# One attention and feed-forward layer on one core: the query products of a half together in slot 5, the key products in slot 6

## What is computed

```python
x1 = x + attention(layernorm(x), ctx)        # q = xn @ w_q, k = ctx @ w_k, v = ctx @ w_v
                                             # softmax(q k^T / 8) v, heads joined, @ w_o + b_o
y  = layernorm(x1)
g  = top2(softmax(y @ gate)), normalised
out = x1 + sum_e g_e * (relu(y @ W1_e + b1_e) @ W2_e + b2_e)
```

## Time and profile before

| | |
|---|---|
| median of 3 runs | 1590.04 us (1586.91 to 1590.92) |
| profiled execution | 1587.79 us, span 1586.0 us |
| busy in the span | PE 1547.8 us, PEld 1444.4, DVE 1265.9, ACT 1102.6, POOL 883.1 |
| granted clock of TensorE, mean | 0.995 of 2.4 GHz |
| DMA | 161.65 MB, mean 102 GB/s |

### The profile page before, as it was taken

One profiled execution on the slowest core, in us unless ns is written; L12 is line 12 of the kernel. 1 busy time (PEld: TensorE's weight loads), 2 busy tenths in 40 slices (PEclk: granted clock), 3 DMA queues, 4 the chain that ended last, 5 costly groups with the idle time before them and its releaser, 6 DMA issues.

```text
span 1586.0 us, 45542 instructions
## 1 busy us (share of the span) xinstructions
PE 1547.8 (98%) x14030; PEld 1444.4 (91%) x14031; DVE 1265.9 (80%) x3796; ACT 1102.6 (70%) x3357; POOL 883.1 (56%) x946
## 2 busy tenths in 40 slices
PE   8999999999999999999999999999899999999997
PEld 7888899989899988889998989989799999999997
DVE  4788888888888888888888888877788777777775
ACT  5777676677776767767767777667667677777774
POOL 2455655655555665565565555555456555555556
PEclk9999999999999999999999999999999999999999
DMA  6533222232222232322223222221799755555554
GB/s 213 156 93 93 73 73 80 80 113 86 80 73 76 84 93 93 93 73 73 80 83 110 88 78 73 77 74 57 250 238 256 144 88 87 88 85 91 84 84 60
DMA packets 123276, 161.65 MB, mean 102 GB/s; under 512 B 18208, under 2 KB 101280, under 8 KB 122976
## 3 DMA queue, kind: packets, MB, share of 16 engines
q1 hardware_dynamic: 77776, 105.59, 22.1%
q0 software_dynamic: 26816, 37.32, 13.4%
q10 hardware_dynamic: 18640, 18.19, 4.4%
HBM read 93.61 MB, written 67.44 MB: 102 GB/s over the span
## 4 chain that ended last, share of the span: by engine, by line
issue 41%; POOL 24%; DVE 9%; DMA 9%; PE 9%; DVEq 3%; ACT 2%; POOLq 1%; ACTq 1%
DMA out<-stage_room,number 9%; POOL lists L680 7%; POOL prob L687 6%; PE bank_a L1453 4%; DVE hid L1381 3%; DVE stage_room L1398 3%; POOL stage_room L729 2%; POOL stage_room L725 2%; POOL shifted L663 2%; POOL mean_var L666 1%; DVEq L1393 1%; POOL rstd L666 1%; DVEq L1372 1%; PE bank_s L1471 1%; PE bank_v L1486 1%
## 5 line engine op out<-in xcount | busy, mean ns | idle before, releaser
L687 POOL TENSOR_TENSOR prob<-prob,inv 128x512 f32<-128x512 f32 x256 | 298.3, 1165 | 462.0 <-DVE inv L978 460.7
L795 ACT ACTIVATE prob<-bank_s,low 128x128 f32<-128x128 f32 x1024 | 363.2, 377 | 58.4 <-DVE low L973 58.4
L973 DVE TENSOR_REDUCE low<-bank_s 128x4 f32<-128x512 f32 x256 | 175.4, 685 | 120.9 <-PE bank_s L1471 120.8
L753 POOL DMA_INDIRECT out<-stage_room,number x142 | 230.6, 1624 | 53.6 <-issue 53.1
L788 ACT ACTIVATE probt<-bank_t 128x512 f32<-128x512 f32 x256 | 153.6, 600 | 116.2 <-PE bank_t L1460 116.1
L795 ACT ACTIVATION_READ_ACCUMULATOR prob<-bank_s,low 128x1 f32 x1024 | 221.5, 216 | 0.0
L1089 DVE SCALAR_TENSOR_TENSOR stage_room<-xin,wo_t 128x256 f32<-128x256 f32 x480 | 201.2, 476 | 0.0
L823 ACT ACTIVATE ot_h<-bank_v 128x512 fp32r<-128x512 f32 x128 | 77.3, 604 | 147.6 <-PE bank_v L1486 147.6
L907 ACT ACTIVATE hidt_h<-hid 128x512 fp32r<-128x512 f32 x142 | 89.7, 632 | 114.4 <-DVE hid L1381 112.1
L680 POOL DMA_INDIRECT lists<-rows,slot x128 | 149.3, 1166 | 34.1 <-issue 34.1
L1460 PE MATMUL bank_t<-ident,prob 128*128 128x128 f32 x1024 | 161.8, 281 | 5.5 <-POOL prob L687 4.7
(11 more groups left out here) (235 smaller groups left out, 4795.5 us busy)
## 6 DMA issues: line engine op xcount, KB each, us to landing
stage_room<-lists ACTq DMA_DIRECT2D x67, 265.0 KB, 2.9
halves<-stage_room SPq DMA_DIRECT2D x32, 512.0 KB, 4.4
homes<-halves SPq DMA_DIRECT2D x16, 1024.0 KB, 6.8
xin<-in_x SPq DMA_DIRECT2D x32, 256.0 KB, 2.8
xraw<-in_x_t SPq DMA_DIRECT2D x32, 256.0 KB, 3.0
stage_room<-in_x SPq DMA_DIRECT2D x32, 256.0 KB, 3.4
stage_room<-in_w SPq DMA_DIRECT2D x32, 256.0 KB, 4.4
out<-stage_room SPq DMA_DIRECT2D x32, 256.0 KB, 2.9
```

The lines of the kernel that those rows point to most:

```text
L687: pool.tensor_tensor(prob[:, n % 4, :, :], prob[:, n % 4, :, :], wide(inv[:, n % 4, :], P), ALU.mult).then_inc(s_norm.sem, 1)
L753: pool.indirect_dma_start(out, bass.IndirectOffsetOnAxis(ap=number[:, u, b:b + 1], axis=0), ysum[:, u, b, :], None, compute_op=ALU.add).th ...
L795: e = act.activation(prob[:, n % 4, h, :], bank_s[n % 2][:, h * P:(h + 1) * P], ACT.Exp, bias=low[:, n % 4, h:h + 1], scale=-1.0, accum_ou ...
L973: dve.tensor_reduce(low[:, n % 4, :], bank_s[n % 2][:, :].rearrange("p (h k) -> p h k", h=4), AX.X, ALU.min).then_inc(s_low.sem, 1)
```

## The change

The slots of the next pair's products are written in another order. Slot 5 had one query and one key product, and so had slot 6; now slot 5 has both query products and slot 6 both key products. The banks follow the position in the slots: the second product of slot 5 has bank 1 and the first of slot 6 bank 2, as before. No operation is added, left out or changed in size.

```diff
@@ -117,8 +117,8 @@
         [("k11", CUR), ("q11", CUR)],
         [("o1", FROM0)],
         [("v10", CUR), ("v11", CUR)],
-        [("q00", NEXT), ("k00", NEXT)],
-        [("q01", NEXT), ("k01", NEXT)],
+        [("q00", NEXT), ("q01", NEXT)],
+        [("k00", NEXT), ("k01", NEXT)],
         [("v00", NEXT), ("f0", BOTH), ("v01", NEXT)],
     ]
 
@@ -140,7 +140,7 @@
     A_BANKS = 4
 
     BANK_OF = {"q10": 0, "k10": 1, "o0": 2, "k11": 3, "q11": 0, "o1": 1, "v10": 2, "v11": 3,
-               "q00": 0, "k00": 1, "q01": 2, "k01": 3, "v00": 1, "f0": 0, "v01": 2}
+               "q00": 0, "q01": 1, "k00": 2, "k01": 3, "v00": 1, "f0": 0, "v01": 2}
```

## The result

The changed kernel takes **1571.76 us** (median of 5 runs, 1570.14 to 1572.39) against 1589.75 (5 runs, 1585.59 to 1590.92): the ratio is 0.9892, with a 95% interval of 0.9877 to 0.9908, or 18.0 us less. The forecast was 1574, range 1569 to 1583. The profiled execution took 1570.14 us, 17.65 less than that of before; its span is 1568.4 us, 17.7 less (1586.04 to 1568.38).

What follows compares the result with a forecast made beforehand. TensorE, busy 98% of the span, was taken to bound the kernel. 30 stalls x 0.47 (0.23 + 0.24) = 14.1, plus 1.4 in iteration -1, made 15.5 us: median 1574, range 1569 to 1583.

Steps and rivals of the forecast that it cites:

- The stall: Slot 5: TensorE at k00's first matmul (L1514) waits for VectorE's low part of the context (L1203), 0.52 us, 30 times.
- What is late next: Scores of slot 6 wait for unit 5's exponentials, plus 0.15 us; start no earlier than 633.30, so slot 5 gives 0.23.
- the new wait: Ahead of slot 6's scores, TensorE waits for the exponentials of unit 5: 0.05 us in place of the old wait.
- The sign that the prediction set: TensorE's waits after: small ones of L1471 for ScalarE's L795, under 0.1 us each and below 4 us in all.
- the twin case: Exponentials don't hold slot 6's scores: 0.52 us per iteration, 17.0 in all, 1573; chance 0.80 together with the forecast.
- Slot 6: k00 has ten matmuls where q01 had twelve: 0.24 us less per iteration.
- Room behind it: Between unit 7's last exponential and the next slot 0 scores 0.7 us is left, so the gain survives.
- Iteration -1: Once: q01 covers all of k00's 1.40 us stall for the k weights, gaining 1.4 us.
- Iteration 29: No stall at k00; TensorE waits 2.98 us for unit 3's normalisation, GpSimd being late; left as it is.
- The pace of ScalarE: Rival: ScalarE's row of work sets the pace; 0.23 us per iteration, 8.3 in all, 1581.7; chance 0.08.
- the moved wait: Rival: the new wait at slot 6's scores takes all; time as before, 1589 to 1590; chance 0.07.
- The rival in which VectorE's low part falls under a GpSimd instruction: L1203 under GpSimd in every iteration costs 1.53 us each through the shared port lock; 32 slower, 1620; chance 0.05.

Runs made afterwards that it cites:

- e1: Kernel before, with VectorE's low part of the context moved ahead of the second copy of v products in slot 4; 1581.61 us, ratio to before 0.9960.
- e4: Changed kernel with q01 moved from slot 5 to the head of slot 6; 1615.87 us, ratio to before 1.0181.
- e2: Changed kernel with VectorE's low part of the context behind slot 5's minimum and reciprocal, except in iteration -1; 1568.85 us, ratio to before 0.9886.
- e10: Changed kernel in which q01 of iteration -1 also waits for the k weights; 1572.54 us, ratio to before 0.9907.
- e9: Kernel before, with VectorE's low part of the context behind slot 5's minimum and reciprocal; 1607.04 us, ratio to before 1.0123.
- e3: Mirror of the change, both key products in slot 5 and both query products in slot 6; 1634.22 us, ratio to before 1.0296.

## Why the prediction was right

*The stall.* 0.52 from start to start, met at 30 places, and all of it gone: shown by the waits after, in which L1514 is no longer named. That it would not be worth 0.52 was the point of the working, and e1 shows it apart: 0.24 measured, 0.23 worked out.

*What is late next.* The exponentials of unit 5, with 0.15 from ScalarE to TensorE, taken from a single case in iteration 0. After the change the distance is 0.14 to 0.15 all along; e4 and e1 show the same limit under other loads, e2 lifts it. The size of the new wait was off: 0.05 was forecast, and e2 gives 0.14. The sign that the prediction set, waits under 0.1 in TensorE's list, did not come either: the list has none. Most of the miss is q01's 1.60 from its first matmul to the values: it took 622.97 - 621.44 = 1.53. I had scaled it from k00's 1.36, and k00 came out of a stop, where the first matmul is followed by the next only 0.20 later (631.15 and 631.35 in the trace before), not 0.12. These 0.08 belong to the stop too, 0.52 + 0.08 = 0.60, and e1 splits the 0.60 into a new wait of 0.36 and a gain of 0.24. The miss cost the sum nothing, because the exponentials decide, but it made the twin case, scores not held, too small: 0.52 per iteration, where e2 gains 0.61 over the kernel before.

*Slot 6.* 0.24 for two matmuls fewer. 0.47 in all were forecast per iteration; 13.08 / 28 = 0.467 was measured. Taken alone it is the 8.28 against 8.04 from the scores of slot 6 to the next scores of slot 0.

*Room behind it.* 0.7 was forecast between the last exponential of unit 7 and the scores of slot 0; it is 632.17 - (631.05 + 0.27) - 0.15 = 0.70. So ScalarE's stretch doesn't set the pace.

*Iteration -1.* 1.4 forecast, 1.27 measured: q00 started 0.07 later in that run (13.52 against 13.45), for reasons ahead of the change, and v00's second matmul followed its first by 0.33, where it was 0.23 before. From q00's start to the first scores it took 10.15 before and 8.81 after, 1.34 less. e10 shows the stall apart, 1.39.

*What was left out.* Iteration 29 was taken as unchanged, and gave 2.96 between the two profiles; the runs above show that the clock behind its stop comes and goes. The parts that the prediction worked out gave 15.2 of its 15.5 (1.27 in iteration -1, 13.96 in iterations 0 to 28 and 30). The other 2.4 of the span's 17.7 are these 2.96, less 0.54 lost in the rest of the kernel; no step of the prediction earned them, and another pair of traces would have given another sum. The loss of 0.54 is of the size by which this stretch varies: it took 469.46 and 469.74 in the two traces of before, 470.00, 469.75 and 470.20 in the three of the changed kernel. The medians differ by 18.0, with an interval of 14.6 to 19.6, in which the 15.5 lies.

*The rivals.* The pace of ScalarE and the moved wait fell with the 33.87. The rival in which VectorE's low part falls under a GpSimd instruction did not happen in any regular iteration; once again only iteration 29 has it, and e2, which puts the two side by side on purpose, shows a price on both sides and no one waiting. The Trainium skill's rule on the shared port (page SBUF — State Buffer, SBUF: two separate sides), by which the instruction that begins second waits for the first, is borne out in e2: with VectorE's low part begun first GpSimd's normalisation is longer (1.40 against 1.04 to 1.19), and VectorE's next instruction, begun behind the normalisation, ends with it (0.99 against 0.12); but no wait followed from it. The rival's price of 1.53 was read too simply. In the earlier trace rows L1203 begins 0.60 ahead of the normalisation and still is the one that is drawn longer; what the rows don't show is that another GpSimd instruction, the indirect DMA at L680, lies there already from 1041.85 to 1042.84. Which of the two held L1203 was not tested, but a normalisation alone, which takes 1.05, need not cost 1.53.

## What to carry to other kernels

Price a stall by the distance to what is late next, not by its length: here a stop of 0.52 us was worth 0.24, and the other half of the gain came from what the reordering put behind the next meeting point. Between two meeting points of the engines, put ahead the work that needs nothing new, and as much of it as the other engine takes anyway; then let the other engine make first what is waited for first (e2), and do that only together, since the same move alone cost 0.65 per iteration (e9). Read TensorE from start to start, since a list of its waits, made of drawn durations, left out a new wait of 0.14 us in nearly every iteration.

## What the runs showed of the hardware

The granted clock behind a stop of TensorE falls in some runs and holds in others, for the same program in the same place. After the stop of 2.6 to 3.0 us in iteration 29 it was 1.00 over the next 4 us in three of twelve traces and 0.50 to 0.68 in nine (the changed kernel: 1.00, 1.00, 0.65). After the stop of 2.2 us in iteration 0 it was 1.00 in seven and 0.57 to 0.64 in five (the changed kernel: 1.00, 0.57, 0.57). After the stop of 1.7 us that e3 has 30 times it was 0.69 and 0.68 in two cases and 1.00 in the others. The stop of iteration 29 made the iteration of the changed kernel 2.7 to 2.8 us longer than a regular one with the clock kept and 4.3 without; in the two traces of the kernel before, neither of which kept it, 3.5 and 5.2. A single profile can't assign a difference of this size to an edit.

VectorE and GpSimd instructions side by side stretched one another in the pairs shown: GpSimd's normalisation from 1.04 to 1.40 beside a VectorE subtraction begun 0.16 before it, and VectorE's L1069 from 0.12 to 0.99 when it was begun 0.42 behind the normalisation.
